# A fused cross-attention and quantised feed-forward layer: batch 1's token sums and batch 7's gate products put ahead of other steps

## What is computed

```python
emb = layernorm(x) + ctx
q, k, v = emb @ wq + bq, emb @ wk + bk, emb @ wv + bv
ek, ew = exp(k - max(k, tokens)), exp(w - max(w, rows))     # w = pos_bias within 64 tokens, 0 elsewhere
y = sigmoid(q) * (ew @ (ek * v)) / (ew @ ek)
a = layer_norm(y @ wo + bo + emb) * gamma + beta
x = x + tanh(g0) * (layer_norm(relu(a @ w1 + b1) @ w2 + b2 + a) * gamma + beta)
n3 = layernorm(x); xq = round(n3 * 127 / max|n3|)            # per token
hid = silu(xq @ Wg) * (xq @ Wu); hq = round(hid * 127 / max|hid|)
x = x + tanh(g1) * (hq @ Wd)                                 # Wg, Wu, Wd: round(w / mean|w|) in -1..1
```

## Time and profile before

| | |
|---|---|
| median of 3 runs | 508.52 us (507.63 to 509.70) |
| the profiled execution: time / span | 509.66 us / 507.9 us |
| mean granted clock of TensorE | 0.982 of 2.4 GHz |
| busy: TensorE / VectorE / ScalarE / POOL | 483.6 / 437.5 / 374.5 / 248.6 us |

### The profile page before, as it was taken

How to read it: one execution, slowest core, us unless ns; L and a number is a source line. 1 busy time by engine, 2 the same in 40 slices (tenths; PEclk the granted TensorE clock), 3 DMA queues, 4 the chain that set the end, 5 groups by cost and what they waited for, 6 DMA issues and landing times.

```text
span 507.9 us, 9896 instructions
## 1 busy us (share of the span) xinstructions
PE 483.6 (95%) x3088; PEld 400.6 (79%) x3088; DVE 437.5 (86%) x1002; ACT 374.5 (74%) x611; POOL 248.6 (49%) x389
## 2 busy tenths in 40 slices
PE   8898999999999999999999999999999999999593
PEld 8686888988877987788877887788868887897352
DVE  6989988787989899898989799897899888957874
ACT  3583869867778778687878588686768687886874
POOL 7391364189125484248525484247415912656511
PEclk9997999999999999999999999999999999999789
DMA  5863251321112330222312430242113111330001
GB/s 185 184 216 122 43 203 47 62 62 57 53 21 43 97 94 21 43 63 72 95 23 62 84 92 13 43 63 73 53 25 80 65 22 21 63 84 3 21 22 42
DMA packets 64018, 34.72 MB, mean 68 GB/s; under 512 B 41696, under 2 KB 63456, under 8 KB 63968
## 3 DMA queue, kind: packets, MB, share of 16 engines
q1 hardware_dynamic: 63136, 34.09, 26.4%
q10 hardware_dynamic: 832, 0.00, 0.1%
HBM read 20.46 MB, written 4.19 MB: 49 GB/s over the span
## 4 chain that ended last, share of the span: by engine, by line
PE 76%; ACT 8%; DVE 6%; DMA 5%; issue 3%; POOL 1%; SPq 0%; DVEq 0%; ACTq 0%; POOLq 0%
PE ps L2516 47%; PE ps L2676 8%; PE ps L2576 7%; PE ps L2698 4%; DMA w_bit<-place_c 3%; PE ps L2585 3%; PE ps L2533 2%; DMA work<-in_L_xattn_wo_dram 2%; PE ps L2524 2%; DVE cols L1749 1%; PE ps L2593 1%; ACT place_c L1010 1%; DVE work L1743 1%; PE ps L2611 1%; ACT work L993 1%
## 5 line engine op out<-in xcount | busy, mean ns | idle before, releaser
L559 POOL TENSOR_TENSOR mv<-mv,cols 128x2 f32<-128x2 f32 x64 | 13.2, 206 | 162.6 <-DVE mv L1615 162.4
L2516 PE MATMUL ps<-w_hi,h_hi 128*128 128x256 f32 x256 | 75.9, 297 | 0.2
L2516 PE MATMUL ps<-w_lo,h_hi 128*128 128x256 f32 x256 | 71.5, 279 | 0.0
L2516 PE MATMUL ps<-w_hi,h_lo 128*128 128x256 f32 x256 | 71.4, 279 | 0.0
L942 ACT ACTIVATE h_hi<-ps,cols 128x512 fp32r<-128x512 f32 (+1 forms) x72 | 45.5, 637 | 13.6 <-PE ps L2516 8.6
L2516 PE MATMUL ps<-n1T_hi,w_hi 128*128 128x512 f32 (+1 forms) x144 | 54.1, 376 | 0.1
L1669 DVE RECIPROCAL ps<-ps 128x512 f32<-128x512 f32 x16 | 53.7, 3358 | 0.1
L2516 PE MATMUL ps<-n1T_lo,w_hi 128*128 128x512 f32 (+1 forms) x144 | 53.3, 370 | 0.0
L2516 PE MATMUL ps<-n1T_hi,w_lo 128*128 128x512 f32 (+1 forms) x144 | 53.2, 370 | 0.0
L2516 PEld LDWEIGHTS ps<-w_hi,h_hi 128*128 128x128 f32 x256 | 48.2, 188 | 3.3 <-DVE h_lo L1704 1.0
L988 ACT ACTIVATE work<-ps,cols 128x1024 f32<-128x1024 f32 x32 | 35.7, 1116 | 19.1 <-PE ps L2676 10.1
(11 more groups left out here) (186 smaller groups left out, 1493.0 us busy)
## 6 DMA issues: line engine op xcount, KB each, us to landing
x_in<-in_x_dram SPq DMA_DIRECT2D x16, 256.0 KB, 3.0
emb<-in_ctx_dram SPq DMA_DIRECT2D x16, 256.0 KB, 2.9
work<-in_x_dram SPq DMA_DIRECT2D x8, 512.0 KB, 3.7
out_dram<-work SPq DMA_DIRECT2D x16, 256.0 KB, 2.2
work<-in_L_xattn_w_dram SPq DMA_DIRECT2D x2, 1024.0 KB, 9.7
work<-in_L_ffn_w_gate_dram SPq DMA_DIRECT2D x1, 1024.0 KB, 5.5
work<-in_L_ffn_w_up_dram SPq DMA_DIRECT2D x1, 1024.0 KB, 5.6
place_c<-in_L_ffn_w_down_dram SPq DMA_DIRECT2D x1, 1024.0 KB, 7.6
```

What stands on the lines that cost most here:

```text
L2516: last = nc.tensor.matmul(dst, lhsT, rhs, start=(i == 0 and not begun), stop=(i == n - 1 and ends))
```

## The change

Around batch 1: on POOL both `embed(1, p)` go ahead of both `w2_lower`; on TensorE the last attention sums of batch 0 are put in another order (the far parts of num 0, den 0 and num 1 first, den 1 last), the transposes of batch 1's token sums go ahead of the 1-column products, which are split around `keys_T`, and both `queries` come before `max_row` and `total(0)`; on ScalarE `emb_upper` of batch 1 goes ahead of `y_upper(0, 0)`; on VectorE both `gated` go ahead of `inverse`, and `emb_lower` of batch 1 ahead of the second `inverse`. The 1-column products and the first total get bank 5 instead of 7, and `queries(1, 1)` bank 7 instead of 0.

Around the end: `xq_rows(7, 0)`, `gate(7, 0)`, `gate(7, 1)` and `up(7, 0)` go ahead of `down(6, 1)` or `down(6, 2)`, and what feeds them goes ahead on ScalarE and VectorE. ScalarE's `hq_columns(6, 3)` goes behind `silu(7, 1)` and `product_scales(7, 1)`. On VectorE `product_scale(7, 3)` goes ahead of `output(7, 0)` and `output(7, 1)`. Batches 6 and 7 get other banks there.

```diff
-    ("q", 0): (1, 3, 1, 3, 0, 0, 0, 6), ("q", 1): (0, 0, 7, 1, 2, 6, 2, 5), ("S", 0): (4, 5, 2, 7, 3, 7, 3, 4),
+    ("q", 0): (1, 3, 1, 3, 0, 0, 0, 6), ("q", 1): (0, 7, 7, 1, 2, 6, 2, 5), ("S", 0): (4, 5, 2, 7, 3, 7, 3, 4),
...
-TOTAL_BANKS = (7, 6, 7)
-B1_BANK, FAR_BANK = 7, 5
+TOTAL_BANKS = (5, 6, 7)
+B1_BANK, FAR_BANK = 5, 5
...
             rsqrt(1, 0, 1)
+            embed(1, 0)
+            embed(1, 1)
             w2_lower(0)
-            embed(1, 0)
             w2_lower(1)
-            embed(1, 1)
...
             w1_upper(1)
-            y_upper(0, 0)
             emb_upper(1, 0)
             emb_upper(1, 1)
+            y_upper(0, 0)
             sum_of_magnitudes(0)
...
             silu(6, 3)
-            hq_columns(6, 1)
             product_scales(7, 0)
             token_quantise(7, 0)
+            hq_columns(6, 1)
+            xq_columns(7, 0)
             hq_columns(6, 2)
-            quantise(6, 3)
-            xq_columns(7, 0)
             normalise(7, 3, 1)
             silu(7, 0)
-            hq_columns(6, 3)
+            quantise(6, 3)
             token_quantise(7, 1)
             silu(7, 1)
             product_scales(7, 1)
+            hq_columns(6, 3)
             xq_columns(7, 1)
...
             gated(0, 0)
+            gated(0, 1)
             inverse(0, 0)
-            gated(0, 1)
             divided(0, 0)
-            b1_whole()
-            inverse(0, 1)
             emb_lower(1, 0)
             emb_lower(1, 1)
+            inverse(0, 1)
+            b1_whole()
...
             token_max(7, 0)
+            token_scales(7, 0)
             product_scale(6, 2)
-            token_scales(7, 0)
+            tile_stats(7, 3, 2)
+            tile_stats(7, 3, 3)
+            mean_variance(7, 3, 1)
             product(6, 3)
-            tile_stats(7, 3, 2)
             product_scale(6, 3)
             output(6, 1)
-            tile_stats(7, 3, 3)
-            mean_variance(7, 3, 1)
-            output(6, 2)
             token_max(7, 1)
             token_scales(7, 1)
+            output(6, 2)
             product(7, 0)
             product_scale(7, 0)
             output(6, 3)
...
             product(7, 3)
+            product_scale(7, 3)
             output(7, 0)
             output(7, 1)
-            product_scale(7, 3)
...
-            attend(0, "num", 1, 3)
-            attend(0, "den", 0, 3)
             attend(0, "num", 0, 2)
+            attend(0, "den", 0, 3)
             attend(0, "num", 0, 3)
+            attend(0, "num", 1, 3)
+            attend_far(0, "num", 0)
+            attend_far(0, "den", 0)
+            attend_far(0, "num", 1)
             attend(0, "den", 1, 2)
             attend(0, "den", 1, 3)
-            attend_far(0, "num", 0)
-            attend_far(0, "den", 0)
             attend_far(0, "den", 1)
-            attend_far(0, "num", 1)
-            for piece in range(4):
-                beta_w1(piece)
             emb_rows(1, 0)
             emb_rows(1, 1)
+            beta_w1(0)
+            beta_w1(1)
             keys_T(1, 0)
             keys_T(1, 1)
+            beta_w1(2)
+            beta_w1(3)
             queries(1, 0)
+            queries(1, 1)
             max_row(1)
             total(0)
-            queries(1, 1)
             keys_values(1, 0)
...
             hq_rows(6, 1)
+            xq_rows(7, 0)
             down(6, 1)
+            gate(7, 0)
             hq_rows(6, 2)
-            xq_rows(7, 0)
+            gate(7, 1)
+            up(7, 0)
             down(6, 2)
-            gate(7, 0)
+            up(7, 1)
             hq_rows(6, 3)
-            up(7, 0)
-            gate(7, 1)
-            up(7, 1)
+            xq_rows(7, 1)
             down(6, 3)
-            xq_rows(7, 1)
             gate(7, 2)
             up(7, 2)
             hq_rows(7, 0)
-            up(7, 3)
             gate(7, 3)
             down(7, 0)
+            up(7, 3)
```

More of the change, by code:

```diff
@@ L60 @@
     ("g", 5): (0, 0, 0, 0, 0, 0, 0, 1), ("g", 6): (0, 0, 0, 0, 0, 0, 0, 5), ("g", 7): (0, 0, 0, 0, 0, 0, 0, 3),
[1 row of a table removed]
[L62 to L68, removed]
[1 row of a table added]
+    ("xqP", 1): (0, 0, 0, 0, 0, 0, 2, 0), ("gate", 0): (6, 6, 2, 6, 2, 6, 6, 2), ("up", 0): (2, 6, 2, 6, 0, 6, 6, 4),
+    ("hqP", 0): (0, 0, 0, 0, 0, 0, 1, 0), ("down", 0): (5, 4, 5, 4, 6, 1, 1, 0),
+    ("gate", 1): (6, 0, 0, 0, 2, 2, 6, 6), ("up", 1): (6, 0, 0, 0, 2, 2, 4, 2), ("hqP", 1): (0, 0, 0, 0, 0, 0, 1, 1),
+    ("down", 1): (1, 1, 1, 1, 6, 5, 1, 1), ("gate", 2): (2, 6, 2, 6, 0, 6, 6, 4), ("up", 2): (2, 6, 2, 6, 2, 2, 0, 6),
+    ("hqP", 2): (0, 0, 0, 0, 0, 0, 0, 6), ("down", 2): (1, 1, 1, 1, 4, 1, 0, 6),
+    ("gate", 3): (2, 6, 2, 6, 2, 2, 2, 2), ("up", 3): (6, 2, 6, 2, 0, 6, 4, 4), ("hqP", 3): (0, 0, 0, 0, 0, 0, 1, 7),
+    ("down", 3): (2, 6, 2, 6, 5, 7, 1, 7)}
 PAIRED = ("gate", "up")
 EWT_BANKS = (1, 6, 7, 1)
-TOTAL_BANKS = (7, 6, 7)
-B1_BANK, FAR_BANK = 7, 5
+TOTAL_BANKS = (5, 6, 7)
+B1_BANK, FAR_BANK = 5, 5
 class Count:
@@ L2732, in _ @@
             key_sums(0)
+            attend(0, "num", 0, 2)
+            attend(0, "den", 0, 3)
+            attend(0, "num", 0, 3)
             attend(0, "num", 1, 3)
-            attend(0, "den", 0, 3)
-            attend(0, "num", 0, 2)
-            attend(0, "num", 0, 3)
+            attend_far(0, "num", 0)
+            attend_far(0, "den", 0)
+            attend_far(0, "num", 1)
             attend(0, "den", 1, 2)
             attend(0, "den", 1, 3)
-            attend_far(0, "num", 0)
-            attend_far(0, "den", 0)
             attend_far(0, "den", 1)
-            attend_far(0, "num", 1)
-            for piece in range(4):
-                beta_w1(piece)
             emb_rows(1, 0)
             emb_rows(1, 1)
+            beta_w1(0)
+            beta_w1(1)
             keys_T(1, 0)
             keys_T(1, 1)
+            beta_w1(2)
+            beta_w1(3)
             queries(1, 0)
+            queries(1, 1)
             max_row(1)
             total(0)
-            queries(1, 1)
             keys_values(1, 0)
```

## The result

The changed kernel took **510.80 us** (median of 8 runs, 509.87 to 513.08); the kernel before, run beside it on the same chip, 509.53 (8 runs, 507.63 to 510.16). The ratio is **1.0044, 95% interval 1.0029 to 1.0058**: within the 0.5% that counts here as no change, but its whole interval lies above 1, so a small loss is there. The two medians differ by 1.3 us, the interval of the ratio stands for 1.5 to 3.0 us. The profiled execution of the changed kernel took 510.79 us (span 509.0).

The account below looks back on a forecast made before the run. TensorE bounds the kernel; only two half-clock places can change, ended by a relay (batch 1) and VectorE (end). First place -0.3, last 0.3 + 1.8 - 0.8 = +1.3, together +1.0 on 508.52: 509.5 us, range 506.8 to 512.0.

Parts of the forecast that it names:

- Steps 1 and 2: Batch 1, POOL: token sums end at 37.3, 3 us earlier; gate weights' load issued at 42.0, landing at 47.5.
- Step 3: Batch 1: ScalarE's queue waits for the gate load, so keys_values(1, 0) begins at 50.7 instead of 51.19.
- Step 4: Batch 1, TensorE: queries end by 48.1 at the latest, not late for 50.7; first place counted as -0.3 us.
- Steps 5 and 6: Last place: ScalarE's new order delays down(6, 1) to 478.25, gate(7, 0) to 479.95, hq_rows(6, 2) to 481.65.
- Step 7: Last place: product(7, 0) at 486.9 against 486.64, +0.3 us, ends -0.3 and +0.8.
- The rule on transposes: Last place: by it the half clock would end no earlier than before, making Step 7 +0.8.
- rival B: Last place: clock returns as late as before, +1.6, 510.1 us; a second fall adds up to 1; chance 0.20.
- Step 8: Last place: hq_columns(6, 3) behind silu(7, 1) stalls VectorE ahead of output(6, 3), +1.8 us (1.7 to 2.0).
- Step 9: The end: product_scale(7, 3) ahead of the outputs of tiles 0 and 1 saves 0.8 us on VectorE.
- Rival C: Batch 1: clock falls just ahead of keys_values(1, 0) if queries run at full clock, +3.5, 512.0 us; chance 0.15.
- A: Last place: clock returns early or never drops, product(7, 0) 2.4 early, total -1.7, 506.8 us; chance 0.18.
- D: Whole kernel: moves cancel, load a little later, other slack meets the stall, within 0.5 us of 508.5; chance 0.10.

Follow-up runs that it names:

- e1_front: The changed kernel with everything around the end as before, so only batch 1's place changed: 509.69 us, ratio 1.0009 to before.
- e4_w2: The changed kernel with POOL's w2_lower(0) ahead of both embed(1, .): 510.96 us, ratio 1.0040 to before.
- e7_transposes: e5_scale plus 19 and 13 f32 transposes of no use ahead of and behind hq_rows(6, 1): 507.75 us, ratio 0.9977 to before.
- e5_scale: The kernel before with only VectorE's product_scale(7, 3) moved ahead of output(7, 0) and output(7, 1): 508.30 us, ratio 0.9986.
- e3_columns: The changed kernel with ScalarE's hq_columns(6, 3) put back ahead of silu(7, 1): 509.36 us, ratio 1.0014 to before.
- e12_bank: e8_front_w2 with the end of e7_transposes, and the last tile's columns and down product in bank 7 instead of 6: 507.08 us, ratio 0.9968 to before.
- e2_end: The kernel before with only the end (batches 6 and 7) changed: 510.64 us, ratio 1.0039 to before.
- e9_changed_busy: The changed kernel plus useless transposes ahead of hq_rows(6, 1) (19), xq_rows(7, 0) (11) and down(6, 3) (13): 509.78 us, ratio 1.0028 to before.
- e10_columns_busy: e3_columns plus useless transposes ahead of hq_rows(6, 1) (19) and xq_rows(7, 0) (11): 508.40 us, ratio 0.9984 to before.
- e6_matmuls: e5_scale plus 9 and 6 useless 512-column matmuls ahead of and behind hq_rows(6, 1): 508.20 us, ratio 0.9983 to before.
- e8_front_w2: e1_front with POOL's w2_lower(0) ahead of both embed(1, .): 509.11 us, ratio 1.0005 to before.

## Why the prediction was right, and where it was not

The forecast was 509.5 us and no change; 510.80 lies in the range and the ratio within 0.5%. Of the 1.3 us between 509.5 and 510.80 the starting point makes 1.0: I added to 508.52, the median of three runs, and that of eight is 509.53. By the profiled executions I expected +1.0 us and they differ by +1.13 (509.66 to 510.79). By the ratio the loss is about 2 us, twice my sum.

The mechanism that carries the loss, the stall ahead of `output(6, 3)`, was right in place, cause and size. That the sum of the profile came out within 0.15 us is partly luck: `product(7, 0)` came 0.7 us earlier than forecast, and the first place, the stall and the scale were together worse by about as much. Step by step:

- *Steps 1 and 2, POOL and the load.* The sums ended at 37.8, not 37.3: POOL waited for a transfer of the context until 35.28 and both halves then took 2.54 us. Before, that transfer was covered by `w2_lower`, and step 1 left it out. The issue came at 42.49 instead of 42.0 (41.9 to 42.1 in four other profiles). The load took 5.7 us; I had assumed 5.5.
- *Step 3, who waits.* The chain is the one I named, 0.5 to 0.7 us later throughout: `keys_values(1, 0)` 51.38 against 50.7 (50.76 in e1_front). e4_w2, which brings the issue forward by 2.3 us, brings it to 50.20. That the load had taken the half clock's place on the path is so shown.
- *Step 4, the queries.* In the profile of after they began at 43.83 and ended at 49.1, a microsecond later than my limit, since TensorE had dropped to half clock within the 1-column products. They were not late for ScalarE. First place: -0.3 predicted; +0.25 at key block 2 in the profile, -0.03 at `up(6, 3)`, -0.4 to +1.3 in the runs of e1_front. Its sign is open.
- *Steps 5 and 6* stand within 0.15 us: `down(6, 1)` 478.20 for 478.25, `gate(7, 0)` 479.86 for 479.95, `hq_rows(6, 2)` 481.57 for 481.65, `hq_columns(6, 2)` 482.67 for 482.55.
- *Step 7, `product(7, 0)`.* I took the middle between two clocks, 486.9. It was 486.24, my value for a clock that returns at 482.7. So +0.3 was -0.4. The rule on transposes that I weighed there, and which made rival B +0.8, isn't borne out: the clock came back 3.2 us earlier, and in e7_transposes it stayed at 1.00 from 476 to 482 us, where e5_scale, the same kernel without the added transposes, has 0.72. (The Trainium skill, "TensorE: Matmul & The Clock Gate", Part 4, says that transposes don't count as TensorE being busy in the way matmuls do; these rows show the opposite.)
- *Step 8, the stall*: 1.94 us for 1.8, at the place and with the releaser that I named, and e3_columns takes 1.4 us of it back with one move.
- *Step 9, the scale first*: I booked -0.8. "Prod to last" went from 18.14 to 19.66, that is +1.52; less the 2.01 us by which `output(6, 3)` came later after `product(7, 0)`, it is -0.5. The sign was right, the size too large by 0.3. It also rested on a term that I didn't name, the move of the last columns to bank 7: without it the same step gained nothing in the profiles (18.16 in e5_scale), with it 0.6 us (17.53 in e12_bank against 18.14 before).
- *What the sum left out* is a second fall of the clock, which stood in rival B. The profile of after doesn't have it. Those of e2_end and e4_w2, which have the same order there, do: with 2 us of idle time ahead of `down(6, 3)` their "prod to last" is 20.76 and 20.77 instead of 19.66. **So step 8 may be too small: I priced the new gap by ScalarE's times alone, and not by what it can do to the clock behind it.** Whether this makes up the difference between my sum and the ratio is open, and the runs of the changed kernel don't speak for it. The mean granted clock of its eight executions is 0.983 to 0.989. A further fall like that of e2_end (0.72 over 6 us) would, by my estimate, bring the profiled 0.984 to 0.981. The three slowest (511.67, 512.48 and 513.08 us) have 0.989, 0.987 and 0.984, the two fastest 0.984. What makes its slow executions slow isn't shown.
- *Rivals A, B and D* did not come. The clock fell (0.50 from 476 to 482 us) and `product(7, 0)` came 0.4 us early, not A's 2.4; the clock came back well ahead of B's; and no slack met the stall, as D had it.
- *Rival C, the clock falling ahead of `keys_values(1, 0)`*, had 0.15; I priced the fall itself at 2.5 us, of a total of 3.5. In the profiles of e9_changed_busy, e10_columns_busy and e12_bank it happened, under the condition named: queries at full clock. Timeline of TensorE, e9_changed_busy:

```profile
45.53 0.40 PE L2516 MATMUL ps<-embT_hi,wq_lo 128*128 128x512 f32 x1
48.11 0.71 PE L2550 MATMUL ps<-ident,cols 128*128 128x128 f32 x4 [2.18 <-DVE cols L1634]
...
50.92 0.77 PE L2516 MATMUL ps<-wkv_hi,embT_hi 128*128 128x512 f32 x1 [0.77 <-ACT work L902]
51.49 0.63 PE L2516 MATMUL ps<-wkv_lo,embT_hi 128*128 128x512 f32 x1
```

  and its stretch behind that:

```profile
52.00:54.00 2.00, 2.00 (x7) 1.62 (x6) 0.79 (x2) 2.00 (x4) 0.00 (x0) 0.50 0.01 4
```

  Key block 2 came at 64.26 to 64.39 in these three, at 62.43 to 63.30 in the other six profiles with the changed first place, with or without e12_bank's `w2_lower`. So the mechanism exists; it costs 1 to 2 us, not 2.5, and not in every execution. e3_columns had its queries partly at full clock (0.76 over 42 to 49 us) and no fall behind them. It is a likely reason why the first place gains nothing in the runs. The other is that it gains little to begin with: in the five profiles with the first place of before, key block 2 lies at 62.75 to 63.93, a range that overlaps that of the six. Neither was tried by itself.

## What to carry to other kernels

When an engine waits for the end of a relay, moving its own work earlier moves the wait to the next runner: here a load behind POOL, and then, with the load early, a product behind queries at half clock. Before a step is put behind another on a queue, work out when its reader will need it: one step behind a `silu` on ScalarE cost 1.4 us. A new gap of 2 us on TensorE is to be priced twice, for itself and for the clock of the work behind it, which fell in three of the four profiles that have this gap (e2_end, e4_w2 and e9_changed_busy, not the changed kernel's). And look at which bank the last steps share: the scale put first on VectorE gained nothing on the last tile's way until two numbers in the bank table were changed, and then 0.6 us.

## What I had not expected

- The stretch at half clock is not a property of the kernel. From 476 to 482 and from 482 to 488 us the granted clock was 0.50 and 0.67 before, and with the same order there 0.50 and 0.69 in e1_front, 0.50 and 0.91 in e8_front_w2, 0.72 and 1.00 in e5_scale. In the changed kernel it was 0.50 and 0.93. In the profiles of e6_matmuls and e8_front_w2 one more began near 500 us and put 0.9 to 1.0 us on "prod to last": the last `down` took 1.86 us instead of 1.03.

```profile
501.67 1.86 PE L2698 MATMUL ps<-wdT,w_bit 128*128 128x256 bf16 x8 [1.30 <-ACT w_bit L1001]
```

- The part that no edit touches and that is at full clock throughout is not constant: from key block 2 to `up(6, 3)` it took 406.6 us in e9_changed_busy, 407.99 before. That alone is a spread of 1.4 us, more than the effect of most edits here.
- 19 f32 transposes of 128 columns took 2.29 us at full clock, 13 took 3.02 at half clock: 0.12 and 0.23 us each.
